# LSTM step 1's recurrent product in three fp16 products, and the splits around it in another order

## The reference

```
def rnn_step(prev_h, xw):              # xw = x[t] @ Wx + b
    next_h = jnp.tanh(prev_h @ Wh + xw)

def lstm_step(prev_h, prev_c, xw_t):   # xw_t = y[t] @ Wx + b, width 2048
    a = xw_t + prev_h @ Wh
    i, f, o = sigmoid(a[:, :H]), sigmoid(a[:, H:2*H]), sigmoid(a[:, 2*H:3*H])
    g = tanh(a[:, 3*H:])
    next_c = f * prev_c + i * g
    next_h = o * tanh(next_c)

y   = x + rnn(x)
out = y + lstm(y)
```

## Time and profile before

| | |
|---|---|
| median of 3 runs | 838.41 us (838.35 to 840.22) |
| the profiled execution: its own time | 839.34 us |
| its span in the profile | 837.5 us |
| TensorE busy | 822.3 us, 98% of the span |
| VectorE, ScalarE, GpSimd busy | 648.0, 612.3, 331.5 us |
| chain that ended last | PE 86%, DVE 5%, DMA 4%, ACT 3% |

### The profile page before, as it was taken

How to read it: one execution, slowest core, us unless ns; L and a number is a source line. 1 busy time by engine, 2 the same in 40 slices (tenths; PEclk the granted TensorE clock), 3 DMA queues, 4 the chain that set the end, 5 groups by cost and what they waited for, 6 DMA issues and landing times.

```text
span 837.5 us, 52092 instructions
## 1 busy us (share of the span) xinstructions
PE 822.3 (98%) x22620; PEld 611.0 (73%) x22620; DVE 648.0 (77%) x1794; ACT 612.3 (73%) x1637; POOL 331.5 (40%) x693
## 2 busy tenths in 40 slices
PE   7899999999999999999999999999999999999997
PEld 4555555677777887777777777777777777777796
DVE  3689778877898777878888787888878787767764
ACT  4896576766778778787877878787787878777752
POOL 1222466734544334343433434343343434333310
PEclk9999999999999999999999999999999999999999
DMA  8711101110011111111111111111111101011001
GB/s 294 266 52 27 29 15 28 29 29 23 11 29 30 29 31 27 42 42 35 46 30 35 26 42 42 33 47 34 29 30 42 42 21 37 17 33 26 13 8 28
DMA packets 54580, 36.21 MB, mean 43 GB/s; under 512 B 9788, under 2 KB 52944, under 8 KB 53072
## 3 DMA queue, kind: packets, MB, share of 16 engines
q1 hardware_dynamic: 54096, 32.78, 14.3%
q10 hardware_dynamic: 256, 0.11, 0.0%
HBM read 19.21 MB, written 8.39 MB: 33 GB/s over the span
## 4 chain that ended last, share of the span: by engine, by line
PE 86%; DVE 5%; DMA 4%; ACT 3%; issue 2%; SPq 0%; ACTq 0%; DVEq 0%
PE ps_l L1602 33%; PE ps_l L1677 27%; PE ps_r L1803 9%; PE ps_l L1655 5%; PE ps_pk L1786 3%; PE ps_end L1786 2%; PE ps_r L1823 2%; PE ps_l L1615 2%; DMA whl_raw<-in_L_cond_Wh 2%; DMA wxl_raw<-in_L_cond_Wx 2%; DMA wxr_raw<-in_L_cond_Wx 1%; DVE wxl_lo L1354 1%; ACT wxl_hi L879 0%; ACT wxl_lo L857 0%; DVE fc L1379 0%
## 5 line engine op out<-in xcount | busy, mean ns | idle before, releaser
L594 POOL TENSOR_TENSOR xb<-xb,h_l 128x128 f32<-128x128 f32 x127 | 58.2, 458 | 379.6 <-DVE h_lo L1414 371.3
L1677 PE MATMUL ps_l<-whl_raw,wxl_raw 128*32 128x256 f16 x3816 | 131.8, 273 | 0.0
L1602 PE MATMUL ps_l<-whl_hi,hT_hi 128*32 128x512 f16 x1888 | 122.6, 379 | 0.0
L1602 PE MATMUL ps_l<-whl_lo,hT_hi 128*32 128x512 f16 x1888 | 122.5, 379 | 0.0
L1602 PE MATMUL ps_l<-whl_hi,hT_lo 128*32 128x512 f16 x1888 | 122.5, 379 | 0.0
L1677 PE MATMUL ps_l<-wxl_hi,wxl_raw 128*32 128x256 f16 x2544 | 115.9, 273 | 0.5 <-ACT ps_l L842 0.5
L1677 PEld LDWEIGHTS ps_l<-whl_raw,wxl_raw 128*32 128x32 f16 x3816 | 102.2, 97 | 2.2
L1602 PEld LDWEIGHTS ps_l<-whl_lo,hT_hi 128*32 128x32 f16 x1888 | 50.8, 97 | 51.2
L1602 PEld LDWEIGHTS ps_l<-whl_hi,hT_lo 128*32 128x32 f16 x1888 | 50.8, 97 | 51.2
L998 ACT ACTIVATE gates<-ps_l,g_products 128x256 f32<-128x256 f32 x115 | 54.1, 470 | 46.5 <-PE ps_l L1602 46.5
L1677 PEld LDWEIGHTS ps_l<-wxl_hi,wxl_raw 128*32 128x32 f16 x2544 | 68.4, 97 | 18.3 <-ACT ps_l L842 1.0
(11 more groups left out here) (263 smaller groups left out, 1925.1 us busy)
## 6 DMA issues: line engine op xcount, KB each, us to landing
xb<-in_x SPq DMA_DIRECT2D x128, 64.0 KB, 2.1
...
```

What stands on the lines that cost most here:

```text
L594: nc.gpsimd.tensor_tensor(xb[g % NX][:, t, :], xb[g % NX][:, t, :], h_l[s % 2][:, :], ALU.add).then_inc(out_done, 1)
L1602: last = nc.tensor.matmul(ps_l[s % 4][quarter(j), :], (hT_hi, hT_lo)[h_part][:, k, :], gate_slice(whl[w_part][k], j), start=False, stop=(h ...
L1677: last = nc.tensor.matmul(at[quarter(j), :], stationary, weights[:, j, :, :], start=False, stop=(y_part == 1 and k == 1), skip_group_check ...
```

## The change

`N0` goes from 2 to 1: LSTM step 1 takes h in halves. Its product starts with the two parts that need the high halves of WhL alone, and takes the low halves chunk by chunk. For it VectorE makes three chunks of WhL's low halves in tick 6 and one in tick 7, and the bound of WxL's chunk 1 goes from tick 6 to tick 7. VectorE takes two peaks of x from ScalarE (groups 2 and 3, in ticks 7 and 8). The low halves of WxL's chunk 3 go from tick 10 to tick 11, those of the RNN's WhR from tick 11 to tick 12, `turn_x(4)` from tick 12 to tick 13. ScalarE makes WhR's high halves in tick 11 behind the tanh of the RNN instead of in tick 10. The first input product in halves (step 5) is cut in three: its high by high part ahead of `recurrent_r(11)`, one chunk behind two thirds of `recurrent_l(5)` in tick 12. The RNN's blocks are split in ticks 35, 36 and 37 (one, two and one chunk) instead of 36 and 38.

The core of the diff (`...` marks what is left out):

```diff
-N0 = 2
+N0 = 1
...
-        TURN_X_AT.update({4 * g - 4: g for g in range(3, GX)})
+        TURN_X_AT.update({4 * g - 4: g for g in range(3, GX) if g != 4})
+        TURN_X_AT[13] = 4
+        TURN_X_AT[LAG] = 2
...
-        W_LOW_AT = {6: [(OF_H, 0), (OF_H, 1)], 7: [(OF_H, 2), (OF_H, 3)], 9: [(OF_X, 1)], 10: [(OF_X, 2)]}
-        W_LOW_LATE_AT = {8: [(OF_X, 0)], 10: [(OF_X, 3)]}
-        W_PEAK_AT = {6: 1}
-        R_LOW_AT = {5: OF_X, 11: OF_H}
-
-        PEAK_ON_ACT_AT = {3: [1], 7: [2], 8: [3], 9: [4], 10: [5, 6, 7]}
...
-        R_HIGH_AT = {5: OF_X, 10: OF_H}
+        W_LOW_AT = {6: [(OF_H, 0), (OF_H, 1), (OF_H, 2)], 7: [(OF_H, 3)], 9: [(OF_X, 1)], 10: [(OF_X, 2)], 11: [(OF_X, 3)]}
+        W_LOW_LATE_AT = {8: [(OF_X, 0)]}
+        W_PEAK_AT = {7: 1}
+        R_LOW_AT = {5: OF_X, 12: OF_H}
+
+        PEAK_ON_ACT_AT = {3: [1], 9: [4], 10: [5], 11: [6, 7]}
+        PEAK_LATE_AT = {7: 2, 8: 3}
...
+        R_HIGH_AT = {5: OF_X}
+        R_HIGH_LATE_AT = {11: OF_H}
...
-        XW_HALVES_AT = {36: (0, 1), 38: (2, 3)}
+        XW_HALVES_AT = {35: (0,), 36: (1, 2), 37: (3,)}
...
+                if k in R_HIGH_LATE_AT:
+                    rnn_weight_high(R_HIGH_LATE_AT[k])
                 for g in PEAK_ON_ACT_AT.get(k, []):
                     peak_by_act(g)
...
                 m = s + 1 - N0
                 if m == 1:
-                    pe.wait_ge(w_split[OF_H], J)
+                    pe.wait_ge(w_high[OF_H], J)
                 pe.wait_ge(lstm_hT_hi, m)
-                for h_part, w_part in ((0, 0), (0, 1), (1, 0)):
+                for h_part, w_part in parts:
                     if h_part == 1:
                         pe.wait_ge(lstm_hT_lo, m)
                     for k in range(J):
+                        if m == 1 and w_part == 1:
+                            pe.wait_ge(w_split[OF_H], k + 1)
...
+                if k - LAG == S1:
+                    recurrent_l(S1, ((0, 0), (0, 1)))
+                elif k - LAG == 1:
+                    recurrent_l(1, ((0, 0), (1, 0), (0, 1)))
+                elif 1 < k - LAG < S3:
                     recurrent_l(k - LAG)
...
+                if k - LAG == S1:
+                    first_of_halves(2)
+                    recurrent_l(S1, ((1, 0),))
+                if k - LAG + 1 == S1:
+                    first_of_halves(0)
...
+                if k == LAG + 1:
+                    next_product_r(k)
                 if LAG < k < R0:
                     recurrent_r(k)
...
                 if k - LAG + 1 == S1:
-                    product_l(S1)
+                    first_of_halves(1)
```

74 lines of the change are left out of this document (48 added, 26 removed).

## The result

| | median (range), runs | ratio to before, 95% interval |
|---|---|---|
| before | 838.75 us (836.28 to 840.22), 21 | |
| changed | 841.15 us (838.82 to 843.31), 21 | 1.0029 (1.0023 to 1.0036) |

The changed kernel is 2.4 us slower, 0.3% by its median. The forecast was 839.0 with a range to 840.2: the result lies outside it, by 1.0 us, on the slow side, where rivals 2 and 3 stood, but by neither's mechanism. The profiled execution has a span of 840.5 and its own time is 842.25, 1.1 above the median.

The account below looks back on a forecast made before the run. TensorE, busy 98% of the span at full clock, was taken to bound the kernel. +0.4 us at the start and +0.2 for the RNN's blocks gave +0.6; forecast 839.0 us, range 836.9 to 840.2.

Parts of the forecast that it names:

- rivals 2 and 3: VectorE bounds ticks 36 to 38, 840.0 us, chance 0.17; and the clock falls, 843.4 us, chance 0.02.
- The second seed in tick 6 (0.6 on ScalarE) lies in its wait for the DMAs.: Tick 6: ScalarE's added seed of 0.6 us fits into idle time and was costed at nothing.
- Part 1: LSTM step 1 in halves: 0.83 us less TensorE work, 0.15 of it left after a new 0.7 us wait.
- Part 2: Ticks 7 to 9: VectorE is late, TensorE waits for hT_hi at `recurrent_l(2)`; +0.4 us, bounds +0.1 and +0.6.
- the chain of VectorE that follows: Low half, cell, halves of h and peaks' diagonal on VectorE leave +0.4 us at `recurrent_l(3)` and `recurrent_l(4)`.
- Part 3: Ticks 11 and 12: hT_r wait gone (-1.0 us), new 1.2 us wait at `turn_peaks`; start +0.4 us in all.
- rival 1: The peaks are in time for `turn_peaks` of tick 12 and the start gains: 837.3 us, chance 0.28.
- Part 4: RNN's blocks: `copy_m1` wait gone (-0.5 us), low halves in ticks 35 and 37 delay `recurrent_l`; net +0.2.
- Rival 2: VectorE becomes the bound in ticks 36 to 38, both 0.64 us delays arriving undiminished: 840.0 us, chance 0.17.
- The check at the end of the prediction: Tick 12: `product_l(6)` was expected near 79.0 us; a start before 78.5 would refute the `turn_peaks` wait.
- rival 4: The change does all it could, work and waits go and nothing comes: 835.8 us, chance 0.03 (elsewhere 0.02).

Follow-up runs that it names:

- before_again: The kernel before, unedited, profiled once more; 838.62 us, ratio 1.0004.
- after_again: The changed kernel, unedited, profiled once more; 841.62 us, ratio 1.0037 to before.
- before_extra_seed: The kernel before with one dead activation of a seed's size added on ScalarE in tick 6; 839.42 us, ratio 1.0009.
- seed_later: The changed kernel with ScalarE's second seed of tick 6 behind WhL's high half of chunk 1; 840.70 us, ratio 1.0026 to before.
- peaks_back: The changed kernel with the peaks of x's groups 2 and 3 on ScalarE again; 839.80 us, ratio 1.0014 to before.
- thirds_only: The kernel before with the change's order from tick 10 and step 5's product in three, peaks 6 and 7 ahead of WhR's high halves; 837.76 us, ratio 0.9989.
- peaks_first: The changed kernel with the peaks of groups 6 and 7 ahead of WhR's high halves in tick 11; 839.66 us, ratio 1.0015 to before.
- all_four: The changed kernel with peaks_back, peaks_first, chunk 1's high half in tick 5 and the RNN's blocks as before; 838.80 us, ratio 1.0007 to before.

## Why the prediction was wrong

The ledger of the profiles, before_again against after_again, from h_r(6) to h_r(35): 201.80 and 204.16, +2.36 us; the RNN's blocks add 0.11. Together that is the 2.4 to 3.1 us of the medians. I had +0.6. The mechanisms that I named were nearly all there; the missing 1.8 us is three terms, one of them costed at nothing.

- **"The second seed in tick 6 (0.6 on ScalarE) lies in its wait for the DMAs."** This is the step that failed, 0.9 us. I took VectorE's c of step 0 at 42.2 from the profile of before and kept it for the changed kernel. In that profile TensorE and its DMAs set it. In most profiles ScalarE and VectorE set it: from h_r(6) to `fc` 8.03 us before, 8.82 in the change (0.6 for the seed, 0.1 for a wider scale of y, the rest on VectorE behind). So the 0.93 that I had `recurrent_l(1)` gain (43.35 for 44.28) is 0.02 (B: 10.79 for 10.81). Shown from both sides: before_extra_seed +0.59 in A, seed_later -0.41.
- **Part 1, the saved work and the new wait.** Predicted 0.7 of wait, measured 0.60 with 0.2 until the pipeline ran again. The low half took 2.48 beside GpSimd, not 2.3: the 0.15 that I left to the upper bound came. The Trainium skill (SBUF — State Buffer, section on two separate sides) has the later of the two fully blocked while the other holds the lock; GpSimd's add had started 0.13 us ahead of the low half at 46.07 and had 0.33 to go, and the low half took 0.15 more, half of my estimate by that rule. From `recurrent_l(1)` to `recurrent_r(8)` it is 7.69 us: 51.0 was predicted for a `recurrent_l(1)` at 43.35, which is 7.65. Right.
- **Part 2, VectorE late.** Right in kind and place, the size short by 0.4. hT_hi's wait stands at `recurrent_l(2)`, 0.62 us. From `recurrent_l(1)` to `recurrent_l(2)` 9.95 was predicted and is 10.25: the cell's second product took 0.55 instead of 0.3, as it did in the trace of before (0.54), where I had gone by the mean of all. To `recurrent_l(3)` it is 19.14 where 18.7 was predicted. That "the chain of VectorE that follows" leaves +0.4 was a claim without a row behind it. By peaks_back the peaks of 2 and 3 are 0.8 of the 1.7 by which C is longer than before.
- **Part 3, the waits of ticks 11 and 12.** The 0.99 is gone, and the wait behind `turn_peaks` is there with the accumulator's read behind it: right, against rival 1. It is 1.7 and not 1.2. From gates to tanh I had 1.5 in step 4; it is 75.70 - 73.46 = 2.24, since y's low half (0.57) and two products of 0.54 stand on VectorE: 0.7 too short. ScalarE's queue from the tanh to the peaks was 0.2 shorter than I had it and TensorE came 0.1 later after the gates, which leaves the 0.5. With that, `product_l(6)` is 36.6 us behind `recurrent_l(1)` (35.7 predicted). The moves out of ticks 11 and 12 that I costed at nothing may not be free: hT_r_lo comes about 0.15 us late near 97 us in after_again, and D has that 0.15 in it. Which piece does it was not tried; thirds_only has the same tables there and not the wait.
- **Part 4, the blocks.** Net +0.2 predicted, +0.1 measured; the wait for `copy_m1` is gone. Of the two hT_hi waits one shows, 0.51 at `recurrent_l(31)`. Right. Rival 2 is out.
- **The check at the end of the prediction** read "if `product_l(6)` starts before 78.5, part 3 is wrong". It starts at 82.04 and 80.0: the sum failed upwards, for which I had named no test.
- **Sums that don't come out as written.** Part 3's list (0.83 and 1.0 less, 0.7, 0.4, 0.15 and 1.2 more) gives +0.6; the +0.4 is 79.05 less 78.63. The list leaves out the 0.2 us that before spent on the hand-over to step 5's recurrent product. Rival 1 takes off the 0.2 of part 4, which has to be added (837.7, not 837.3), and rival 4 has 0.03 in one place and 0.02 in another. None of this decides the result.

The sum again with the measured terms: 0.6 + 0.9 (the head start that was not there) + 0.4 (VectorE) + 0.5 (the peaks) = 2.4. TensorE was indeed "later than I have it", as rival 1 needed (0.4 us after `recurrent_l(1)`), but ScalarE was later by more (0.8). The range failed since each of the three had a bound of a few tenths at most, and no bound allowed for idle time that is there in one execution and not in another.

What stays open: the medians of peaks_first and peaks_back fell by 0.3 to 1.0 us more than their profiles show, while all_four, which has both, fell by 2.4 to 2.8 with 2.15 in its profile. With 11 or 12 runs each I can't tell this from chance; the part of the run behind h_r(127) alone varies by 1.0 us.
